# Selective scan and quantized MLP on one core: second-half states added on GpSimd, whole-row peak and square, gating behind the scan, five more products on VectorE

## The chip, the core and the metric

The kernel runs on one core of a Trainium2 chip. A core has five engines that run their own instruction streams and meet only at semaphores: TensorE (PE in the profile), VectorE (DVE), ScalarE (ACT), GpSimd (POOL) and SyncE (SP, which issues the DMAs). The metric is the device time of one execution in microseconds. The lower, the better.

## The reference, cut to what matters

The kernel computes one gated cross-attention-like block. `x` has 4 batches of 512 rows and 512 columns. First a Mamba layer reads a context, then a quantized gated MLP follows:

```python
# Mamba: state [d_inner = 512, 16] for each batch, 512 time steps
def step(state, inp):
    d, b, c, u = inp
    dA = jnp.exp(d[..., None] * A)
    state = state * dA + (d * u)[..., None] * b[:, None, :]
    y = jnp.einsum('bdn,bn->bd', state, c)
    return (state, y)
...
# MLP of 2048 columns; each row is scaled by its RMS and its largest magnitude
xn = rmsnorm(x)
scale = 127.0 / jnp.clip(jnp.max(jnp.abs(x), axis=-1, keepdims=True), EPS, None)
...
h = jax.nn.silu(bitlinear(x, w1)) * bitlinear(x, w2)
return bitlinear(h, w3)
```

`bitlinear` rounds its input rows to integers from -128 to 127 and its weights to -1, 0 and 1. For the third product each row of `h` therefore needs its largest magnitude and its mean square.

## The kernel before, in words

**Steps.** The scan is cut into 128 steps, 32 for each batch, numbered k. A step is a tile `hh[k % 6]` of 128 partitions by 1024 elements. In batches 0 and 1 it holds two states over 512 times. In batches 2 and 3 (`SPLIT`) it holds four states over 256 times: the first 16 steps of such a batch (k = 64 to 79 and 96 to 111) do the first half of the time, the last 16 (k = 80 to 95 and 112 to 127) the second half. Each step passes through these operations:

1. `times_b` on GpSimd (L702, L708): `hh` = (d·u)·B. It waits until TensorE has consumed step k-6 (`s_sum`), since `hh` has six buffers.
2. `exp` on ScalarE (L736, L743): the decay into one of two PSUM tiles `da`, after the scan of step k-2 has freed it.
3. `scan` on VectorE (L763 to L774): the recurrence along the free dimension. In a first half, column 0 of each state's decay is zero, so one instruction of 1024 elements handles four states. In a second half the state at the middle of the time must come in: `keep_state` on ScalarE has copied it into `hl`, and the scan is four instructions of 256 elements, each with its own initial value from `hl` (L770).
4. `times_c` on GpSimd (L813, L818): `hh` = `hh`·C. For the steps in `BY_VECTOR` the scan writes into `da` instead and VectorE multiplies (`times_c_vector`, L796); `exp` of step k+2 then waits for that product.
5. `sums` on TensorE (L851): eight transposes that add into `bank_y`.

**Order.** Every engine's order is written out by hand in slots k. In slot k, GpSimd does `times_c(k)` and `times_b(k+4)`, VectorE does `scan(k+3)`, ScalarE `exp(k+4)`, TensorE `sums(k-1)`.

**MLP tiles.** The 16 row tiles of the MLP start at the slots of `TILE` (38, 44, 50, 56, 70, 76, 82, ..., 118 for the first 13). From slot `tile_slot(i)` on, TensorE makes chunk c (512 of 2048 columns) in slot +c: `a_tensor` (L1020) waits until VectorE has read the chunk before out of `bank_a`, `b_tensor` (L1029) until it has read `bank_b`. In slot +c+1, ScalarE takes a tanh (L1041) and VectorE does two instructions (`gated_vector`, L1048 and L1054), which before stand **ahead of** the slot's scan. ScalarE squares chunks 0 and 1 in slot +2 and chunks 2 and 3 in slot +4 (L1059) and turns each into a part of the mean square `v2` (L1068). VectorE takes the largest magnitudes in the same two halves (L1093). GpSimd raises `v2` to the power -1/2 in slot +7 (`rh_pool`, L1127). VectorE derives the two scales from it (`scales_vector`, L1106 to L1116) and ScalarE rounds `h` (L1123). Tiles 13 to 15 run after the last slot, with code of their own.

Of the kernel before, what the change touches and what calls it, by code (L numbers as in the profile page):

```python
# [13 lines left out]
P = 128  # L14
# [48 lines left out]
BY_VECTOR = (14, 16, 25, 45, 49, 53, 62, 67, 68, 73, 77)  # L63
# [30 lines left out]
def build(nc, book, x, ctx_t, in_w, xp_w, dt_w, weights, consts, out):  # L94
    u_dram = nc.dram_tensor("u_scratch", [NB, P, NE, L], F32).ap()
    xd_dram = nc.dram_tensor("xd_scratch", [NB, ROWS, L], F32).ap()
    with ExitStack() as ctx:
# [23 lines left out]
        sm = sb("sm", [P, 282])  # L121
# [53 lines left out]
        col = iter(range(282))  # L175
# [18 lines left out]
        am1, ram1, rh, rk_most, rk_am, csh = [small() for _ in range(6)]  # L194
# [18 lines left out]
        HA = line("state_scalar")  # L213
# [7 lines left out]
        hl = sb("hl", [P, NE, NS])  # L221

# [466 lines left out]
        def times_b(g_, k):  # L689
# [6 lines left out]
            if split(k):  # L696
                b, h, q, n = where_split(k)
                t = slice(HALF * h, HALF * (h + 1))
                if h == 0 and q == 0:
# [4 lines left out]
                                           [P, 4, HALF]), bb[:, n:n + 4, t], ALU.mult)  # L704
            else:
# [4 lines left out]
            ins.then_inc(s_m1, 1)  # L710

        def exp(act, k, parts=(0, 1)):
# [16 lines left out]
            if split(k):  # L729
                b, h, q, n = where_split(k)  # L730
                da = quarters(flat(dbank[k % 2]))
                if 0 in parts and (k % PER < 2 or h == 0 and c_by_vector(k - 2)):
                    act.activation(da[:, :, 0], zero4[:, :], ACT.Copy)
                first = 1 - h
                for j in [2 * part + i for part in parts for i in range(2)]:
                    ins = act.activation(da[:, j, first:HALF],  # L736
                                         dt2[g % 4][:, HALF * (q % 2) + first:HALF * (q % 2 + 1)], ACT.Exp,
                                         scale=a_neg[:, q, n + j:n + j + 1])
# [6 lines left out]
            if 1 in parts:  # L745
                ins.then_inc(s_exp, 1)

# [10 lines left out]
        def scan(v, k):  # L758
# [297 lines left out]
        def square_scalar(act, i, c):  # L1056

            act.wait_ge(*MV.of(("h", i, c)))
            MA.did(act.activation(view(room, 4096, 1024), h_at(i)[:, c - 1:c + 1, :].rearrange("p a b -> p (a b)"),  # L1059
                                  ACT.Square, accum_out=ssq[:, c // 2:c // 2 + 1]), ("sq", i, c))  # L1060
            act.wait_ge(*MA.now())
            if c == 1:
                act.wait_ge(*MA.of(("k2", rows_by(i))))
            mean_square(act, i, c // 2, c == 3)
# [26 lines left out]
        def peak_vector(v, i, half):  # L1091
            v.wait_ge(*MV.of(("h", i, 2 * half + 1)))
            MV.did(v.tensor_reduce(amh[:, half:half + 1], h_at(i)[:, 2 * half:2 * half + 2, :].rearrange(  # L1093
                "p a b -> p (a b)"), AX.X, ALU.max, apply_absolute_value=True), ("peak", i, half))

        def v2_at(i):
            return ssv[:, 2:3] if at_end(i) else ssv[:, 1:2]

        def scales_vector(v, i, part):
            t = i % NE  # L1100
            if part == 0:
                v.wait_ge(*MV.of(("peak", i, NCH - 1 if at_end(i) else 1)))
                if at_end(i):
                    MV.did(v.tensor_scalar(am1, amh[:, 0:1], amh[:, 1:2], amh[:, 2:3], ALU.max, ALU.max))
                else:
                    MV.did(v.tensor_scalar(am1, amh[:, 0:1], amh[:, 1:2], None, ALU.max))  # L1106
# [108 lines left out]
        def out_vector(v, i):  # L1215
            t = i % NE
            v.wait_ge(*MP.of(("o", i)))
            MV.did(v.scalar_tensor_tensor(out=x2_at(i), in0=bank_g(i)[:, :], scalar=fin[i % 2], in1=x2_at(i),
# [10 lines left out]
        with nc.Block() as block:  # L1229
# [147 lines left out]
            def _(g_):  # L1377
# [37 lines left out]
                for k in range(80, SLOTS):  # L1415
                    for i in range(END):
                        if k == tile_slot(i) + 7:
                            rh_pool(g_, i)
                    if k < ALL and not c_by_vector(k):
                        times_c(g_, k)  # L1420
                    for first, n, done in TURNS:
# [5 lines left out]
                rh_pool(g_, 12)  # L1427
# [16 lines left out]
            def _(act):  # L1444
# [62 lines left out]
                for k in range(38, 80):  # L1507
# [24 lines left out]
                    for i in range(END):  # L1532
                        if k == tile_slot(i) + 7:
                            hq_scalar(act, i, 0)
                            hq_scalar(act, i, 1)
                    for i in range(END):
                        if k == tile_slot(i) + 2 or k == tile_slot(i) + 4:
                            square_scalar(act, i, k - tile_slot(i) - 1)
# [12 lines left out]
                    for first, n, done in TURNS:  # L1551
                        if k == done + 5:
                            rows_scalar(act, first, min(n, END - first))
                            if first + n > END:
                                rows_scalar(act, END, 1)
                for k in range(80, SLOTS):
# [3 lines left out]
                    for i in range(END):  # L1560
                        c = k - tile_slot(i) - 1
                        if 0 <= c < NCH:
                            tanh_scalar(act, i, c)
                    if k + LEAD < ALL:
                        exp(act, k + LEAD)
                    if k + LEAD - 2 < ALL:
# [8 lines left out]
                    for i in range(END):  # L1575
                        if k == tile_slot(i) + 7:
                            hq_scalar(act, i, 0)
                            hq_scalar(act, i, 1)
                    for i in range(END - 1):
# [10 lines left out]
                    for i in range(END):  # L1590
                        if k == tile_slot(i) + 2 or k == tile_slot(i) + 4:
                            square_scalar(act, i, k - tile_slot(i) - 1)
# [9 lines left out]
                    for b in range(NB):  # L1602
                        if k == (13, 34, 66, 94)[b]:
                            z_scales(act, b)
                act.preload_act_table_set("silu_and_others")
# [427 lines left out]
```

## Time and profile before

| | us |
|---|---|
| median of 3 runs | 653.23 (653.22 to 656.8) |
| the profiled execution: its own time | 653.69 |
| its span, first to last instruction | 651.9 |
| DVE busy in the span | 583.0 (89%) |
| ACT busy | 530.7 (81%) |
| POOL busy | 587.9 (90%) |
| PE busy | 488.3 (75%) |

The profile is of one execution. "Busy" is the time in which an engine had an instruction under way. A wait is the idle time just ahead of an instruction, put down to the event that came last. The page also follows the chain of work that ended last; it gives 30% of the span to POOL, 29% to DVE, 14% to ACT and 11% to PE. POOL's record begins its dense part at 26.93 us and ends its last `times_c` at 607.66 us.

### The profile page before, as it was taken

The numbers are of one execution on the slowest core, as the hardware profiler recorded it, in microseconds if no ns is written. First come the engines' busy times: TensorE is split into PE (matmuls) and PEld (weight loads), VectorE is DVE, ScalarE is ACT, GpSimd is POOL, SyncE is SP. The second block draws the span as 40 slices with busy tenths as digits, with TensorE's granted clock in tenths as the row PEclk, the third lists the DMA queues.
The fourth block names the chain that finished last, engine by engine and source line by source line (L and its number), as shares of the span: only waits on it lengthen the run. The fifth ranks groups of instructions, "written<-read, shape, count | busy, mean of one in ns | idle before, by whom it ended". The sixth has DMA issues, their size and how long they took to land.

```text
span 651.9 us, 7928 instructions
## 1 busy us (share of the span) xinstructions
PE 488.3 (75%) x2560; PEld 296.4 (45%) x2560; DVE 583.0 (89%) x772; ACT 530.7 (81%) x969; POOL 587.9 (90%) x289
## 2 busy tenths in 40 slices
PE   8798878994564678777666486778676887668987
PEld 3254434552553445455534354455454554345543
DVE  6779779997998899999999999989997999999765
ACT  5764767788999778987798797899999898897675
POOL 1399999998999999999999999999999999999431
PEclk9988999997555979999786889889989897978999
DMA  5598587579960100147420100037700000000001
GB/s 186 193 407 309 183 329 276 198 270 389 374 262 0 39 1 2 47 153 276 132 78 0 33 2 17 1 127 244 254 37 1 17 1 18 0 16 18 1 17 48
DMA packets 24472, 80.77 MB, mean 124 GB/s; under 512 B 2464, under 2 KB 5152, under 8 KB 21360
## 3 DMA queue, kind: packets, MB, share of 16 engines
q1 hardware_dynamic: 24432, 80.27, 33.9%
q8 instruction: 20, 0.33, 0.2%
q14 instruction: 20, 0.16, 0.1%
HBM read 72.53 MB, written 7.73 MB: 123 GB/s over the span
## 4 chain that ended last, share of the span: by engine, by line
POOL 30%; DVE 29%; ACT 14%; issue 13%; PE 11%; DMA 2%; SPq 0%; DVEq 0%; POOLq 0%; ACTq 0%
POOL hh L708 15%; POOL hh L818 14%; DVE hh L773 9%; DVE hh L770 8%; DVE room L1048 4%; ACT da L736 3%; DVE sm L1093 2%; PE bank_a L1020 2%; PE bank_b L1029 2%; PE bank_y L851 2%; ACT room L1041 1%; PE da L1211 1%; DVE bank_y L576 1%; DVE sm L904 1%; ACT gbuf L922 1%
## 5 line engine op out<-in xcount | busy, mean ns | idle before, releaser
L773 DVE TENSOR_TENSOR_SCAN hh<-da,hh 128x1024 f32<-128x1024 f32 x85 | 193.4, 2280 | 3.1 <-ACT da L743 3.0
L851 PE MATMUL bank_y<-ident,hh 128*128 128x128 f32 x1024 | 145.3, 292 | 10.8 <-POOL hh L818 8.8
L851 PEld LDWEIGHTS bank_y<-ident,hh 128*128 128x128 f32 x1024 | 129.6, 152 | 40.1 <-issue 17.5
L813 POOL TENSOR_TENSOR hh<-hh,cc 128x1024 f32<-128x1024 f32 x60 | 141.0, 2350 | 0.2 <-ACT hl L756 0.2
L818 POOL TENSOR_TENSOR hh<-hh,cc 128x1024 f32<-128x1024 f32 x57 | 134.2, 2355 | 0.0
L708 POOL TENSOR_TENSOR hh<-pair,bb 128x1024 f32<-128x1024 f32 x30 | 70.5, 2352 | 26.4 <-DMA bb<-xd_scratch 24.2
L770 DVE TENSOR_TENSOR_SCAN hh<-da,hl,hh 128x256 f32<-128x256 f32 x128 | 85.4, 729 | 0.0
L708 POOL TENSOR_TENSOR hh<-wq,bb 128x1024 f32<-128x1024 f32 x32 | 75.3, 2357 | 1.8 <-PE bank_y L851 1.8
L702 POOL TENSOR_TENSOR hh<-wq,bb 128x1024 f32<-128x1024 f32 x32 | 75.1, 2346 | 0.3 <-PE bank_y L851 0.3
L702 POOL TENSOR_TENSOR hh<-pair,bb 128x1024 f32<-128x1024 f32 x32 | 75.2, 2355 | 0.0
L736 ACT ACTIVATE da<-wq,cst 128x256 f32<-128x256 f32 x128 | 53.3, 463 | 12.0 <-DVE hh L770 11.6
L743 ACT ACTIVATE da<-pair,cst 128x511 f32<-128x511 f32 x64 | 41.3, 679 | 23.3 <-DVE hh L773 23.3
L1020 PE MATMUL bank_a<-wq,room 128*128 128x512 fp8e4 x120 | 34.2, 412 | 30.2 <-DVE room L1048 27.4
L736 ACT ACTIVATE da<-pair,cst 128x255 f32<-128x255 f32 x128 | 53.0, 459 | 3.5 <-DVE hh L773 3.4
L743 ACT ACTIVATE da<-wq,cst 128x511 f32<-128x511 f32 x64 | 41.4, 682 | 9.4 <-DVE hh L773 9.2
L1020 PE MATMUL bank_a<-wq,xqT 128*128 128x512 fp8e4 x112 | 32.4, 417 | 21.7 <-DVE room L1048 21.7
L1041 ACT ACTIVATE room<-bank_a,sm 128x512 f32<-128x512 f32 x58 | 39.0, 673 | 9.0 <-PE bank_a L1020 8.9
L1211 PE MATMUL bank_t<-wq,room 128*128 128x512 fp8e4 x192 | 45.0, 389 | 0.1
L1048 DVE SCALAR_TENSOR_TENSOR room<-room,bank_a 128x512 f32<-128x512 f32 x52 | 35.2, 677 | 8.0 <-ACT room L1041 7.6
L1029 PE MATMUL bank_b<-wq,room 128*128 128x512 fp8e4 x120 | 34.1, 411 | 0.0
L1190 ACT ACTIVATE room<-bank_t,sm 128x1024 bf16<-128x1024 f16 (+1 forms) x28 | 30.4, 1085 | 4.4 <-PE bank_t L1173 4.4
L987 PE MATMUL bank_t<-ident,room 128*128 128x128 f16 x56 | 6.1, 238 | 34.2 <-ACT room L969 17.4
(271 smaller groups left out, 1051.7 us busy)
## 6 DMA issues: line engine op xcount, KB each, us to landing
bb<-xd_scratch SPq DMA_DIRECT2D x32, 512.0 KB, 5.1
cc<-xd_scratch SPq DMA_DIRECT2D x32, 512.0 KB, 6.9
wq<-weights SPq DMA_DIRECT2D x12, 1024.0 KB, 6.5
stage<-weights SPq DMA_DIRECT2D x8, 1024.0 KB, 6.1
xin<-x SPq DMA_DIRECT2D x4, 1024.0 KB, 5.4
room<-weights SPq DMA_DIRECT2D x4, 1024.0 KB, 8.2
u_scratch<-wq SPq DMA_DIRECT2D x6, 512.0 KB, 3.0
wq<-x SPq DMA_DIRECT2D x2, 1024.0 KB, 18.8
```

The source lines that it names most:

```text
L702: ins = g_.tensor_tensor(quarters(flat(hh[k % NH])), du2[g % 4][:, HALF * (q % 2):HALF * (q % 2 + 1)].unsqueeze(1).to_broadcast([P, 4, HAL ...
L708: ins = g_.tensor_tensor(hh[k % NH][:, :, :], du2[g % 4].unsqueeze(1).to_broadcast([P, GN, L]), bb[:, s * GN:(s + 1) * GN, :], ALU.mult)
L736: ins = act.activation(da[:, j, first:HALF], dt2[g % 4][:, HALF * (q % 2) + first:HALF * (q % 2 + 1)], ACT.Exp, scale=a_neg[:, q, n + j:n ...
L743: ins = act.activation(dbank[k % 2][:, j, 1:L], dt2[g % 4][:, 1:L], ACT.Exp, scale=a_neg[:, q, s * GN + j:s * GN + j + 1])
L770: ins = v.tensor_tensor_scan(to[:, t], da[:, t], h[:, t], hl[:, q, n + j:n + j + 1], ALU.mult, ALU.add)
L773: ins = v.tensor_tensor_scan(to, da, h, 0.0, ALU.mult, ALU.add)
L813: ins = g_.tensor_tensor(quarters(flat(hh[k % NH])), quarters(flat(hh[k % NH])), cc[:, n:n + 4, t], ALU.mult)
L818: ins = g_.tensor_tensor(hh[k % NH][:, :, :], hh[k % NH][:, :, :], cc[:, s * GN:(s + 1) * GN, :], ALU.mult)
L851: mm = pe.matmul(bank_y[:, (first + c) * P:(first + c + 1) * P], flat(hh[k % NH])[:, at:at + P], ident[:, :], start=False, stop=(s == STEP ...
L1020: mm = pe.matmul(a[:, :], xqT[i % 2][:, k, :], w1q[:, k, c * 512:(c + 1) * 512], start=(k == 0), stop=(k == NE - 1))
L1048: MV.did(v.scalar_tensor_tensor(out=th[c % 2], in0=th[c % 2], scalar=1.0, in1=a[:, :], op0=ALU.add, op1=ALU.mult), ("g", i, c))
L1211: mm = pe.matmul(bank_g(i)[:, :], hqT[:, f, :], w3q[:, f, :], start=(f == 0), stop=(f == KF - 1))
```

## The change

In the steps of a second half the scan becomes one instruction of 1024 elements, as in a first half. The state from the middle of the time is brought in ahead of it: ScalarE computes `gain`, the decay of the first column, once for each split batch (`state_gain`, 4 instructions of 128x16, kept in a part of `ones`); GpSimd multiplies `hl` by it once for each group of 128 channels (`carried`, 4 in a batch) and adds the four values of a step to the first column of each state in `hh` (`add_state`, 16 in a batch). It is now `add_state`, and no longer `times_b`, that lets the scan go. Column 0 of the decay is zero throughout, and ScalarE computes 255 columns where it computed 256.

Peak and square of tiles 0 to 12 are one instruction of 2048 elements each, in slot +4. `rh_pool` moves from slot +7 to +6. Two small products move from VectorE to ScalarE (`rk_scalar`, `fin_scalar`), and VectorE makes the scale with three instructions instead of six. `gated_vector` stands behind the scan of its slot. Five steps more (42, 58, 90, 104, 117) have their product by C on VectorE.

```diff
-BY_VECTOR = (14, 16, 25, 45, 49, 53, 62, 67, 68, 73, 77)
+BY_VECTOR = (14, 16, 25, 42, 45, 49, 53, 58, 62, 67, 68, 73, 77, 90, 104, 117)
...
+        gain = ones[:, 0:NE * NS].rearrange("p (e n) -> p e n", e=NE)
...
+                if h:
+                    HG.did(ins, ("product", k))
+                    return
...
+        def carried(g_, k):
+            b, h, q, n = where_split(k)
+            if n == 0:
+                g_.wait_ge(*HA.of(("gain", b)))
+                g_.wait_ge(*HA.of(PER * b + 4 * q + 3))
+                HG.did(g_.tensor_tensor(hl[:, q, :], hl[:, q, :], gain[:, q, :], ALU.mult), ("carried", k))
+
+        def add_state(g_, k):
+            b, h, q, n = where_split(k)
+            g_.wait_ge(*HG.of(("product", k)))
+            first = quarters(flat(hh[k % NH]))[:, :, 0]
+            g_.tensor_tensor(first, first, hl[:, q, n:n + 4], ALU.add).then_inc(s_m1, 1)
...
+        def state_gain(act, b):
+            if b == SPLIT[0]:
+                act.wait_ge(*WP.of("total"))
+            else:
+                act.wait_ge(*HG.of(("carried", PER * (b - 1) + PER - 4)))
+            for q in range(NE):
+                g = NE * b + 2 + q // 2
+                ins = act.activation(gain[:, q, :], a_neg[:, q, :], ACT.Exp,
+                                     scale=dt2[g % 4][:, HALF * (q % 2):HALF * (q % 2) + 1])
+            HA.did(ins, ("gain", b))
...
-            if split(k) and where_split(k)[1]:
-                b, _, q, n = where_split(k)
-                for j in range(4):
-                    t = slice(HALF * j, HALF * (j + 1))
-                    ins = v.tensor_tensor_scan(to[:, t], da[:, t], h[:, t], hl[:, q, n + j:n + j + 1],
-                                               ALU.mult, ALU.add)
-            else:
-                ins = v.tensor_tensor_scan(to, da, h, 0.0, ALU.mult, ALU.add)
-            ins.then_inc(s_scan, 1)
+            v.tensor_tensor_scan(to, da, h, 0.0, ALU.mult, ALU.add).then_inc(s_scan, 1)
...
-        def square_scalar(act, i, c):
+        def square_scalar(act, i):
+            act.wait_ge(*MV.of(("h", i, NCH - 1)))
+            MA.did(act.activation(view(room, 4096, 1024).bitcast(BF16), h_all(i), ACT.Square,
+                                  accum_out=ssq[:, 0:1]), ("sq", i))
...
+        def peak_vector(v, i):
+            v.wait_ge(*MV.of(("h", i, NCH - 1)))
+            MV.did(v.tensor_reduce(am1, h_all(i), AX.X, ALU.max, apply_absolute_value=True), ("peak", i))
...
+        def rk_scalar(act, i):
+            act.wait_ge(*MG.of(("rh", i)))
+            MA.did(act.activation(rk, rh, ACT.Copy, scale=kk[:, i % NE:i % NE + 1]), ("rk", i))
+
+        def scale_vector(v, i):
+            v.wait_ge(*MV.of(("peak", i)))
+            v.wait_ge(*MA.of(("rk", i)))
+            MV.did(v.tensor_scalar(hm, am1, rk, 1e-5, ALU.mult, ALU.max), ("hm", i))
+            v.wait_ge(*MV.now())
+            MV.did(v.reciprocal(hinv, hm))
+            v.wait_ge(*MV.now())
+            MV.did(v.tensor_scalar(csh, hinv, rk, 127.0, ALU.mult, ALU.mult), ("csh", i))
...
@@ GpSimd, slots 80 and on
-                        if k == tile_slot(i) + 7:
+                        if k == tile_slot(i) + 6:
                             rh_pool(g_, i)
                     if k < ALL and not c_by_vector(k):
                         times_c(g_, k)
+                    if second_half(k + LEAD - 1):
+                        add_state(g_, k + LEAD - 1)
+                    if second_half(k + LEAD):
+                        carried(g_, k + LEAD)
...
@@ VectorE, slots 38 and on
+                    if k + LEAD - 1 < ALL:
+                        scan(v, k + LEAD - 1)
                     for i in range(END):
                         c = k - tile_slot(i) - 1
                         if 0 <= c < NCH:
                             gated_vector(v, i, c)
-                    if k + LEAD - 1 < ALL:
-                        scan(v, k + LEAD - 1)
```

In ScalarE's slots from 80 on, a step of `BY_VECTOR` now has its state kept ahead of the `exp` that waits for it, and not behind.

The order of GpSimd in slots 81 to 83, where tile 5 (slot 76) has its `rh_pool`. Before (L702 is `times_b`, L813 `times_c`, L1127 `rh_pool`):

```order
L813 TENSOR_TENSOR hh<-hh,cc 128x1024 [waits s_scan]
L702 TENSOR_TENSOR hh<-wq,bb 128x1024 [waits s_sum]
L813 TENSOR_TENSOR hh<-hh,cc 128x1024 [waits s_scan]
L702 TENSOR_TENSOR hh<-wq,bb 128x1024 [waits s_sum]
L1127 TENSOR_TENSOR sm<-sm 128x1 [waits s_mlp_scalar]
L813 TENSOR_TENSOR hh<-hh,cc 128x1024 [waits s_scan]
```

With the change (L704 `times_b`, L837 `times_c`, L732 `add_state`, L1167 `rh_pool`), slots 81 and 82:

```order
L837 TENSOR_TENSOR hh<-hh,cc 128x1024 [waits s_scan]
L732 TENSOR_TENSOR hh<-hh,hl 128x4 [waits s_state_pool]
L704 TENSOR_TENSOR hh<-wq,bb 128x1024 [waits s_sum]
L1167 TENSOR_TENSOR sm<-sm 128x1 [waits s_mlp_scalar]
L837 TENSOR_TENSOR hh<-hh,cc 128x1024 [waits s_scan]
L732 TENSOR_TENSOR hh<-hh,hl 128x4 [waits s_state_pool]
```

Each slot has a small addition more, behind the product by C, and `rh_pool` stands a whole slot (two large products) earlier.

The order of VectorE in slot 116, the fourth chunk of tile 11. Before (L1048 and L1054 are `gated_vector`, L770 the scan, L1093 the peak, L1218 `out_vector`):

```order
L1048 SCALAR_TENSOR_TENSOR room<-room,bank_a 128x512
L1054 TENSOR_TENSOR wq<-room,bank_b 128x512
L770 SCALAR_TENSOR_TENSOR hh<-da,hl,hh 128x256 x4
L1093 TENSOR_REDUCE sm<-wq 128x1
L1218 SCALAR_TENSOR_TENSOR room<-bank_t,sm,room 128x512
```

With the change:

```order
L798 SCALAR_TENSOR_TENSOR hh<-da,hh 128x1024
L1072 SCALAR_TENSOR_TENSOR room<-room,bank_a 128x512
L1078 TENSOR_TENSOR wq<-room,bank_b 128x512
L1119 TENSOR_REDUCE sm<-wq 128x1
L1260 SCALAR_TENSOR_TENSOR room<-bank_t,sm,room 128x512
```

The scan is one instruction and comes first; the two gating instructions follow it.

## Rows read from the trace of the kernel before

**Rows 1.** The page, parts 1 and 2: whole span, busy tenths of 40 slices.

```profile
PE 488.3 (75%) x2560; PEld 296.4 (45%) x2560; DVE 583.0 (89%) x772; ACT 530.7 (81%) x969; POOL 587.9 (90%) x289
...
POOL 1399999998999999999999999999999999999431
```

**Rows 2.** 20 us each: busy PE, PEld, DVE, ACT, POOL; clock, DMA share, GB/s.

```profile
280.00:300.00 20.00, 16.21 (x106) 10.36 (x106) 19.76 (x23) 15.98 (x25) 20.00 (x10) 1.00 0.54 185
...
560.00:580.00 20.00, 13.27 (x73) 8.03 (x72) 19.19 (x37) 16.53 (x38) 20.00 (x11) 0.83 0.03 13
```

**Rows 3.** Waits of POOL, whole span: us in total, times, longest.

```profile
POOL hh L708 <- DMA bb<-xd_scratch: 24.2, 1, 24.2
POOL sm L1127 <- ACT sm L1068: 20.5, 3, 8.3
POOL hh L708 <- PE bank_y L851: 4.0, 3, 1.8
```

**Rows 4.** Timeline of POOL: start, us, instruction, idle before it in brackets.

```profile
574.24 0.53 POOL L1127 TENSOR_TENSOR sm<-sm 128x1 f32<-128x1 f32 x1
574.74 2.34 POOL L813 TENSOR_TENSOR hh<-hh,cc 128x1024 f32<-128x1024 f32 x1
```

**Rows 5.** POOL by line and form: busy us, mean ns of one, idle before.

```profile
L1127 POOL TENSOR_TENSOR sm<-sm 128x1 f32<-128x1 f32 x16 | 8.6, 540 | 20.5 <-ACT sm L1068 20.5
L1133 POOL TENSOR_SCALAR room<-room,sm 128x1024 f16<-128x1024 f32 x3 | 3.4, 1119 | 1.0 <-DVE sm L1115 0.8
...
L928 POOL TENSOR_TENSOR sm<-sm 128x4 f32<-128x4 f32 x2 | 2.0, 1008 | 0.0
L1141 POOL TENSOR_SCALAR wq<-wq,sm 128x512 f16<-128x512 f32 x2 | 1.4, 692 | 0.9 <-DVE sm L1115 0.8
...
L1379 POOL MEMSET wq<- 128x3 f32 x4 | 0.2, 100 | 0.3 <-POOLq L2027 0.3
```

**Rows 6.** DVE by line and form.

```profile
L773 DVE TENSOR_TENSOR_SCAN hh<-da,hh 128x1024 f32<-128x1024 f32 x85 | 193.4, 2280 | 3.1 <-ACT da L743 3.0
L770 DVE TENSOR_TENSOR_SCAN hh<-da,hl,hh 128x256 f32<-128x256 f32 x128 | 85.4, 729 | 0.0
L1048 DVE SCALAR_TENSOR_TENSOR room<-room,bank_a 128x512 f32<-128x512 f32 x52 | 35.2, 677 | 8.0 <-ACT room L1041 7.6
...
L796 DVE TENSOR_TENSOR hh<-da,cc 128x1024 f32<-128x1024 f32 x11 | 13.5, 1225 | 0.4
...
L1115 DVE TENSOR_SCALAR sm<-sm 128x1 f32<-128x1 f32 x16 | 3.4, 214 | 0.6
```

**Rows 7.** ACT by line and form.

```profile
L1068 ACT ACTIVATE sm<-sm 128x1 f32<-128x1 f32 x35 | 13.5, 387 | 1.2
...
L623 ACT ACTIVATE wq<-wq 128x2048 f32<-128x2048 f32 x4 | 7.6, 1904 | 0.0
```

**Rows 8.** Timeline of DVE, end of tile 9's last chunk.

```profile
511.31 2.28 DVE L773 TENSOR_TENSOR_SCAN hh<-da,hh 128x1024 f32<-128x1024 f32 x1
```

**Rows 9.** Timeline of ACT, tile 9's second square.

```profile
511.42 1.06 ACT L1059 ACTIVATE room<-wq 128x1024 f32<-128x1024 f32 x1 [0.28 <-DVE wq L1054]
...
512.61 0.39 ACT L1068 ACTIVATE sm<-sm 128x1 f32<-128x1 f32 x1
```

**Rows 10.** Timeline of POOL beside it.

```profile
512.38 2.35 POOL L813 TENSOR_TENSOR hh<-hh,cc 128x1024 f32<-128x1024 f32 x1
...
517.03 0.53 POOL L1127 TENSOR_TENSOR sm<-sm 128x1 f32<-128x1 f32 x1
```

**Rows 11.** Timeline of PE, chunk 1 of tile 7.

```profile
439.86 1.04 PE L1020 MATMUL bank_a<-wq,xqT 128*128 128x512 fp8e4 x4 [1.31 <-DVE room L1048]
...
441.60 1.04 PE L851 MATMUL bank_y<-ident,hh 128*128 128x128 f32 x8
```

**Rows 12.** Timeline of POOL beside it.

```profile
440.95 2.36 POOL L813 TENSOR_TENSOR hh<-hh,cc 128x1024 f32<-128x1024 f32 x1
443.27 2.35 POOL L702 TENSOR_TENSOR hh<-wq,bb 128x1024 f32<-128x1024 f32 x1
```

More of the change, by code:

```diff
@@ L174, in build @@
         gates = cst[:, 92:94]
-        col = iter(range(282))
+        col = iter(range(285))
         def small(n=1):
@@ L193, in build @@
         ssq, ssv, amh = [small(3) for _ in range(3)]
-        am1, ram1, rh, rk_most, rk_am, csh = [small() for _ in range(6)]
+        am1, ram1, rh, rk, rk_most, rk_am, hm, hinv, csh = [small() for _ in range(9)]
         fin = [small() for _ in range(2)]
@@ L1089, in peak_end, with fin_scalar @@
                    ("peak", i, c))
[L1091 to L1094, printed above, removed]
+        def peak_vector(v, i):
+            v.wait_ge(*MV.of(("h", i, NCH - 1)))
+            MV.did(v.tensor_reduce(am1, h_all(i), AX.X, ALU.max, apply_absolute_value=True), ("peak", i))
         def v2_at(i):
-            return ssv[:, 2:3] if at_end(i) else ssv[:, 1:2]
+            return ssv[:, 2:3] if at_end(i) else ssv[:, 0:1]
+        def rk_scalar(act, i):
[9 more added lines that the diff above has]
+            MV.did(v.tensor_scalar(csh, hinv, rk, 127.0, ALU.mult, ALU.mult), ("csh", i))
+        def fin_scalar(act, i):
+            act.wait_ge(*MV.of(("hm", i)))
+            MA.did(act.activation(fin[i % 2], hm, ACT.Copy, scale=g3d), ("fin", i))
         def scales_vector(v, i, part):
@@ L1101, in scales_vector @@
             if part == 0:
[L1102 to L1106, printed above, removed]
+                v.wait_ge(*MV.of(("peak", i, NCH - 1)))
+                MV.did(v.tensor_scalar(am1, amh[:, 0:1], amh[:, 1:2], amh[:, 2:3], ALU.max, ALU.max))
                 v.wait_ge(*MV.now())
@@ L1217, in out_vector @@
             v.wait_ge(*MP.of(("o", i)))
+            if not at_end(i):
+                v.wait_ge(*MA.of(("fin", i)))
             MV.did(v.scalar_tensor_tensor(out=x2_at(i), in0=bank_g(i)[:, :], scalar=fin[i % 2], in1=x2_at(i),
@@ L1590, in _ @@
                     for i in range(END):
-                        if k == tile_slot(i) + 2 or k == tile_slot(i) + 4:
-                            square_scalar(act, i, k - tile_slot(i) - 1)
+                        if k == tile_slot(i) + 4:
+                            square_scalar(act, i)
+                    for i in range(END):
+                        if k == tile_slot(i) + 6:
+                            rk_scalar(act, i)
                     for i in TILES:
@@ L1884, in _ @@
                             rows_vector(v, first, n)
-                    for i in range(END):
-                        if k == tile_slot(i) + 5:
-                            scales_vector(v, i, 0)
                     for first, n, done in TURNS:
@@ L1906, in _ @@
                             du_vector(v, 2 * n + 1)
-                    for i in range(END):
-                        if k == tile_slot(i) + 2:
-                            peak_vector(v, i, 0)
                 for k in range(80, SLOTS):
@@ L1921, in _ @@
                                 aggr_vector(v, i)
+                    if k + LEAD - 1 < ALL:
+                        scan(v, k + LEAD - 1)
                     for i in range(END):
@@ L1925, in _ @@
                             gated_vector(v, i, c)
-                    if k + LEAD - 1 < ALL:
-                        scan(v, k + LEAD - 1)
-                    for i in range(END):
-                        if k == tile_slot(i) + 5:
-                            scales_vector(v, i, 0)
                     for first, n, done in TURNS:
```

67 lines of the change are left out of this document (40 added, 27 removed).

## Prediction

> **What bounds the kernel now.** Read the page's busy line and its slices first. POOL is busy 90% of the span, but that is no average of a half idle engine: after the start its slices stand at 9 until the last three [rows 1]. The table by stretch shows 20.00 us of 20 for POOL, with DVE at 19.2 to 19.8 and ACT at 16.0 to 16.5 [rows 2]. Then read POOL's waits: 24.2 us once, at the start, for the first rows of B; 20.5 us in three waits for ScalarE's mean squares, which are those of the last three tiles, after the scan; and 4.0 us for TensorE [rows 3]. So from 27 us to 608 us GpSimd issues one large product after another, every 2.32 us (from 440.95 to 443.27) [rows 12], and the end of that stream releases the last sums, from which the tail of some 44 us is counted. The time is the sum of GpSimd's instructions in the dense part, plus its waits. VectorE is nearly as full, though. The chain that ended last passes through it, and it leads GpSimd by a few us only. Less work on DVE alone therefore buys nothing, and less on POOL buys something only as long as DVE keeps its lead.
>
> **The change, on GpSimd.** Removed: five products by C, 5 x 2.32 = 11.6 us. Added: 32 additions of 128x4 and 8 products of 128x16. The trace has no small addition, so it is bounded. From below, by the memset of 128x3, 0.10 us [rows 5]. From above, by the power of 128x1, which takes 0.50 us from start to start (574.24 to 574.74) [rows 4]; that one is mostly the power itself, since four elements take 1008 ns against 540 for one, 0.16 us an element, which leaves 0.38 us fixed [rows 5]. The one-input operation with a pointer scalar takes 1119 ns for 1024 elements and 692 for 512: 0.27 us fixed [rows 5]. An addition needs no pointer scalar and no power routine, but reads two operands; I take 0.20 us, between the memset and that 0.27, nearer to the latter. Then 32 x 0.20 = 6.4 us, and 8 x 0.22 = 1.8 us. Net on POOL: -11.6 + 8.2 = **-3.4 us**. With 0.10 us it is -7.6, with 0.50 it is +8.4.
>
> The Trainium skill (GPSIMD Engine Reference, Elementwise — side-by-side cycle accounting) gives 4497 ns for a two-input addition of 2048 elements. Against the 2.32 us that 1024 elements take here, this leaves an estimated 0.14 us fixed; the additions would come to 5.6 us and the net to -6.0.
>
> **On VectorE.** A second-half scan takes 85.4/32 = 2.67 us in four pieces and 2.28 in one [rows 6]: 32 x 0.39 = -12.5. The scales shrink from six tiny operations to three, at about 0.2 us each (214 ns) [rows 6]: 13 x 0.6 = -7.8. One peak of 2048 for two of 1024 I count as nothing. Five products at 1.225 us [rows 6] add 6.1. Sum -14 us. None of it shows in the time by itself; it enlarges VectorE's lead. It is unevenly spread: up to slot 80 there is no second half, and DVE gets two products (+2.5) against six tiles' scales (-3.6), while GpSimd is relieved of 4.6.
>
> **On ScalarE.** Two squares of 1.06 us with their reading and scaling (0.39 each) become one of 1.90 us (the 2048-wide one) [rows 7, 9]; `rk`, `fin` and eight small exponentials take about that much again. ACT has 3.5 us of 20 idle [rows 2], so zero, apart from the moment at which things are ready.
>
> **The moved steps and what they wait for.** Two moves work against the gain.
>
> First, `gated_vector` behind the scan frees `bank_a` one scan, 2.3 us, later. TensorE is already waiting there (1.31 us before 439.86), and what is queued behind is the sums that free `hh`: in tile 7 they run from 441.60 to 442.64, and GpSimd takes the buffer at 443.27 [rows 11, 12]. Only 0.6 us is left, and 2.3 us more would stall POOL by 1.7, unless DVE's lead has grown by as much. Against this, VectorE no longer stands idle for ScalarE's tanh (7.6 us in all) [rows 6].
>
> Second, `rh_pool` comes a slot earlier while its mean square comes later. Take tile 9: its last chunk will be complete where the scan ends now, at 513.6 [rows 8]; then a square of 1.90, its accumulator read and the scaling of 0.39, some 2.6 us in all, gives 516.2 [rows 7, 9]. GpSimd is at the place where `rh_pool` will stand at 512.38, whereas today it comes to it at 517.03 [rows 10]. At today's relative position it would wait 3.8 us. But such a wait shifts GpSimd once: afterwards it runs that much later behind VectorE, and the next tile finds its value ready, as long as VectorE keeps the lead. VectorE's 12.5 us in second halves supply it, and POOL's additions do too. In slots 38 to 80 there is no such supply; I price the loss there at 2 us, about one shift of the lead, less what the vanished waits for tanh return.
>
> Sum: -3.4 + 2 = -1.4 us. The profiled execution took 653.69, its span 651.9 and 1.8 around it; it stands 0.5 above the median. Against the median of 653.2 the forecast is **651.8 us**.
>
> **The rivals.**
>
> 1. *Cheap additions, and the waits swallowed.* With 0.10 us each and no new wait the sum is -7.6: 645.6. For it: the memset's row, and the idle places of DVE that vanish. Against it: only 0.6 us of slack on the sums. A cost between, near -6, gives 647. Chance 0.25.
>
> 2. *The early `rh_pool` and late square bind in tile after tile.* GpSimd waits in front of `rh_pool` for ScalarE, with `times_c`, `add_state` and so the scan of three steps later behind it. It decides where VectorE's lead can't reach the 3.8 us that tile 9 asks for, because the scan now waits for `add_state`, which comes a product (2.3 us) later than `times_b` did; GpSimd and VectorE then hold each other. Half of that deficit, 1.9 us, on six of the eight tiles from slot 76 on is +11: 653.2 - 3.4 + 11 = 661. For it: the rows of tile 9. Against it: the lead is lost only by product moves, three in that part. Chance 0.12.
>
> 3. *Dear additions.* At 0.40 us the added work is 32 x 0.40 + 8 x 0.42 = 16.2 us, the net +4.6, with the 2 us of waits 659.8. For it: the fixed 0.38 of the power. Chance 0.10.
>
> 4. *The relief cancels.* Moving a product changes the lead by 2.3 + 1.2 = 3.5 us each time, and VectorE becomes the bound up to slot 80, so the first two products give nothing: -3.4 + 4.6 = +1.2, or 654.4. Chance 0.15.
>
> **How the numbers follow.** The forecast has 0.38 of the chance. A measurement here tells about 1% (6.5 us) from no change. Faster by more than that, below 646.7, takes most of rival 1 and a little of the forecast's price range: 0.22. Slower, above 659.8, takes rival 2 and half of rival 3: 0.17. Within: 0.61. The range reaches from rival 1 (645.5) to dear additions with some waits, 659.5.
>
> **What would show it.** Each step in the profile of the changed kernel: POOL's rows for the 128x4 additions (0.20 us apart from start to start); POOL still at 20 of 20 us in stretches from 30 to 600, while DVE falls to about 18 in the second halves; waits of POOL on `bank_y` (sums) and on ScalarE's mean square of a few us before 600, not more than 4 in all; VectorE's waits for the tanh gone; the last `times_c` at about 606 in place of 607.7. The prediction is wrong if the additions take under 0.1 or over 0.4 us, or if POOL shows more than 6 us of new waits ahead of `rh_pool` or `times_b`.

## The result

The changed kernel takes 689.9 us (median of 4 runs, 688.2 to 693.5) against 653.2 before: the ratio is 1.053, with a 95% interval of 1.050 to 1.057. By the ratio it is slower by 35 us, and it lies far above the range that was given. One of the four executions of rh_late, a run told below, took 724.8 us at a granted TensorE clock of 0.71, where its others had 0.87; it is left out.

**The profile after.** The page's busy line and POOL's slices, which answer to [rows 1]:

```profile
PE 502.5 (73%) x2560; PEld 304.3 (44%) x2560; DVE 572.0 (83%) x629; ACT 530.3 (77%) x969; POOL 583.3 (85%) x324
...
POOL 1499999998999698798998799998997799999521
```

VectorE is busy 11.0 us less than before, where 14 was summed, and GpSimd 4.6 us less, where 3.4 was; the span is 34.5 us longer. The three stretches that show it, two of them those of [rows 2] (busy us of PE, PEld, DVE, ACT, POOL; clock; DMA):

```profile
core 0: us, PE busy (x) PEld busy (x) DVE busy (x) ACT busy (x) POOL busy (x), PEclk, DMA share, GB/s
220.00:240.00 20.00, 13.66 (x76) 9.05 (x74) 16.81 (x15) 9.98 (x16) 14.14 (x7) 0.83 0.08 26
280.00:300.00 20.00, 14.80 (x100) 9.43 (x100) 17.43 (x16) 16.44 (x23) 16.51 (x9) 1.00 0.31 106
560.00:580.00 20.00, 14.16 (x80) 8.85 (x80) 17.20 (x17) 14.90 (x31) 20.00 (x15) 0.91 0.03 13
```

In two of the three GpSimd is no longer full: 14.1 and 16.5 us of 20. Where it went is in the waits of POOL, over the whole span, against [rows 3]:

```profile
POOL sm L1167 <- ACT sm L1094: 29.9, 8, 8.3
POOL hh L713 <- DMA bb<-xd_scratch: 23.8, 1, 23.8
POOL hh L713 <- PE bank_y L875: 18.2, 8, 5.9
POOL hh L704 <- PE bank_y L875: 14.1, 8, 4.9
```

The waits for `bank_y` (TensorE's sums) have gone from 4.3 to 32.3 us, those for the mean square from 20.5 to 29.9. VectorE has new waits too:

```profile
DVE bank_y L578 <- PE bank_y L875: 17.7, 8, 4.7
DVE gbuf L532 <- ACT bank_a L526: 14.2, 10, 2.3
DVE hh L798 <- POOL hh L732: 8.3, 7, 2.6
```

`L578` is the y gate, the product of the finished sums with the gated z, which comes every eight slots. It waits 17.7 us for the sums. Before, from 200 to 600 us, it waited 0.7 there. GpSimd's account closes: 28.0 (sums) + 9.4 (mean square) + 1.8 (other) of new waits, less 4.6 of work, is 34.6 us, and the last `times_c` ends at 642.3 in place of 607.7.

**What was right.** The prices of the added work, which the trace before did not have:

```profile
L732 POOL TENSOR_TENSOR hh<-hh,hl 128x4 f32<-128x4 f32 x32 | 6.5, 203 | 0.2
...
L726 POOL TENSOR_TENSOR hl<-hl,ones 128x16 f32<-128x16 f32 x8 | 1.8, 224 | 0.0
```

0.203 us for an addition, where 0.20 was taken, and 0.224 for a product of 128x16, where 0.22 was. The scan and the peak:

```profile
L798 DVE TENSOR_TENSOR_SCAN hh<-da,hh 128x1024 f32<-128x1024 f32 x112 | 254.6, 2280 | 14.8 <-POOL hh L732 8.3 <-ACT da L764 5.1 <-ACT da L757 0.6
...
L1072 DVE SCALAR_TENSOR_TENSOR room<-room,bank_a 128x512 f32<-128x512 f32 x52 | 34.6, 665 | 2.7 <-ACT room L1065 2.6
...
L1119 DVE TENSOR_REDUCE sm<-room 128x1 f32<-128x2048 f32 x7 | 16.0, 2283 | 0.2
```

The second-half scan takes 2.28 us in one piece, and the wait for the tanh at the gating (L1072) has fallen from 7.6 to 2.6 us. Both were forecast. None of it shows in the time, because the engines now wait for each other.

**The loop.** This is the chain of waits in the slots 39 and 40 (start, duration, engine and line), as the chain that ended last has it:

```profile
216.84 1.18 DVE da L798
...
219.05 0.69 DVE room L1072
...
219.78 1.04 PE bank_a L1044 x4
220.82 0.86 PE bank_b L1053 x4
221.68 0.89 PE bank_y L875 x8
...
222.59 0.71 DVE bank_y L578
...
224.00 2.28 DVE hh L798
226.28 0.59 DVE room L1072
...
226.92 1.89 PE bank_a L1044 x4
228.81 1.71 PE bank_b L1053 x4
230.52 1.67 PE bank_y L863 x8
232.18 0.87 PE bank_y L875 x8
```

Read it downwards. The chain gives an instruction only the part that counts in it: the first scan lasts 2.30 us on VectorE. When it ends, the gating (L1072) starts at 219.05, and only that frees `bank_a`. TensorE makes the two MLP products (L1044, L1053), and behind them, in its queue, the sums of slot 39 (L875). The y gate (L578) needs those sums, and scan and gating of slot 40 stand behind the y gate. So the next `bank_a` is free only at 226.87. TensorE, which waited 4.4 us for it, makes two products, the products that start the next group's `bank_y` (L863) and the sums of slot 40, until 233.1. GpSimd wants the buffer of those sums for `times_b`:

```profile
224.92 2.36 POOL L713 TENSOR_TENSOR hh<-pair,bb 128x1024 f32<-128x1024 f32 x1
233.14 2.36 POOL L713 TENSOR_TENSOR hh<-pair,bb 128x1024 f32<-128x1024 f32 x1 [5.86 <-PE bank_y L875]
```

It idles 5.86 us. The same happens in slot 72, where the y gate again meets a tile's second chunk (4.87 us at 381.01).

One link more lies in these rows. The four products for `bank_a` take 1.04 us at 219.78 and 1.89 us at 226.92, after TensorE has idled 4.37 us. The granted clock (third figure from the end) was 1.00 from 216 to 222 us and has fallen to 0.50, the lower of its two levels, during that idle time:

```profile
226.90:229.00 2.10, 2.08 (x5) 0.74 (x6) 2.10 (x2) 0.15 (x1) 0.38 (x1) 0.50 0.00 0
229.00:232.00 3.00, 3.00 (x12) 2.33 (x11) 2.74 (x4) 1.73 (x3) 0.00 (x0) 0.50 0.00 0
```

So the sums come later still. In the kernel before, the products of the same slot, at 221.55, took 1.04 us after 0.73 us of idling. Of the five longest waits of GpSimd for the sums from 200 to 600 us, four (at 233.14, 313.39, 381.01 and 465.59, 16.2 us in all) have such a stretch at 0.50 just ahead of them, and one (3.49 us at 284.39) has none, though TensorE had idled 3.62 us there. At 1.00 the two MLP products and the sums take 2.61 us from the start of the first to the start of what follows (at 281.53). At 226.92 the two MLP products and those of L863 take 5.10 us in its place; at 309.23 and 461.42 the first three groups take 3.87 and 3.92, and at 375.82 all four take 4.95 in place of some 3.48. So I estimate that the lower clock makes 6.5 of those 16.2 us. The mean granted clock from 200 to 600 us is 0.90 before and 0.86 with the change. No run holds the clock fixed, so its part in the 35 us is not shown.

### The profile page after: what moved, and what is told of

Its sections match the earlier page's. It is cut to its first block, busy times and chain, and to the rows that moved or that the text cites. A ratio compares the mean times of both kernels' runs of the same rounds, so it can differ in the third digit from the quotient of the medians.

```text
span 686.4 us, 7829 instructions
## 1 busy us (share of the span) xinstructions
PE 502.5 (73%) x2560; PEld 304.3 (44%) x2560; DVE 572.0 (83%) x629; ACT 530.3 (77%) x969; POOL 583.3 (85%) x324
## 4 chain that ended last, share of the span: by engine, by line
DVE 22%; PE 21%; POOL 18%; issue 17%; ACT 16%; DMA 4%; SPq 1%; DVEq 0%; POOLq 0%; ACTq 0%
POOL hh L704 9%; DVE hh L798 9%; POOL hh L837 7%; PE bank_y L875 3%; PE bank_a L1044 3%; PE bank_b L1053 3%; DMA wq<-x 3%; DVE room L1072 2%; ACT da L764 2%; ACT da L757 2%; PE bank_b L258 2%; DVE da L798 2%; PE bank_t L270 1%; ACT wq L681 1%; PE bank_a L258 1%
## 5 line engine op out<-in xcount | busy, mean ns | idle before, releaser
L798 DVE TENSOR_TENSOR_SCAN hh<-da,hh 128x1024 f32<-128x1024 f32 x112 | 254.6, 2280 | 14.8 <-POOL hh L732 8.3
L875 PE MATMUL bank_y<-ident,hh 128*128 128x128 f32 x1024 | 148.8, 296 | 11.1 <-POOL hh L842 9.0
L875 PEld LDWEIGHTS bank_y<-ident,hh 128*128 128x128 f32 x1024 | 133.3, 155 | 43.4 <-issue 21.0
L837 POOL TENSOR_TENSOR hh<-hh,cc 128x1024 f32<-128x1024 f32 x57 | 134.4, 2359 | 2.0 <-ACT hl L788 2.0
L842 POOL TENSOR_TENSOR hh<-hh,cc 128x1024 f32<-128x1024 f32 x55 | 129.8, 2361 | 0.0
L704 POOL TENSOR_TENSOR hh<-pair,bb 128x1024 f32<-128x1024 f32 x32 | 75.5, 2362 | 8.8 <-PE bank_y L875 8.8
L704 POOL TENSOR_TENSOR hh<-wq,bb 128x1024 f32<-128x1024 f32 x32 | 75.4, 2356 | 5.3 <-PE bank_y L875 5.3
L1044 PE MATMUL bank_a<-wq,room 128*128 128x512 fp8e4 x120 | 39.3, 460 | 40.8 <-DVE room L1072 36.5
L764 ACT ACTIVATE da<-pair,cst 128x511 f32<-128x511 f32 x64 | 41.3, 680 | 20.5 <-DVE hh L798 20.5
L757 ACT ACTIVATE da<-wq,cst 128x255 f32<-128x255 f32 x128 | 53.3, 467 | 2.0 <-DVE hh L798 2.0
L1044 PE MATMUL bank_a<-wq,xqT 128*128 128x512 fp8e4 x112 | 33.3, 425 | 21.3 <-DVE room L1072 20.9
L1251 PE MATMUL bank_t<-wq,room 128*128 128x512 fp8e4 x192 | 43.4, 379 | 0.8 <-ACT room L1230 0.8
L1053 PE MATMUL bank_b<-wq,room 128*128 128x512 fp8e4 x120 | 38.9, 457 | 0.0
L798 DVE TENSOR_TENSOR_SCAN da<-da,hh 128x1024 f32<-128x1024 f32 x16 | 36.6, 2288 | 1.5 <-ACT da L764 1.2
L1072 DVE SCALAR_TENSOR_TENSOR room<-room,bank_a 128x512 f32<-128x512 f32 x52 | 34.6, 665 | 2.7 <-ACT room L1065 2.6
L1044 PEld LDWEIGHTS bank_a<-wq,room 128*128 128x128 bf16 x120 | 11.5, 110 | 55.3 <-DVE room L1072 40.1
```

What stands on the lines that cost most here:

```text
L704: ins = g_.tensor_tensor(quarters(flat(hh[k % NH])), du2[g % 4][:, HALF * (q % 2):HALF * (q % 2 + 1)].unsqueeze(1).to_broadcast([P, 4, HAL ...
L757: ins = act.activation(da[:, j, 1:HALF], dt2[g % 4][:, HALF * (q % 2) + 1:HALF * (q % 2 + 1)], ACT.Exp, scale=a_neg[:, q, n + j:n + j + 1])
L764: ins = act.activation(dbank[k % 2][:, j, 1:L], dt2[g % 4][:, 1:L], ACT.Exp, scale=a_neg[:, q, s * GN + j:s * GN + j + 1])
L798: v.tensor_tensor_scan(to, da, h, 0.0, ALU.mult, ALU.add).then_inc(s_scan, 1)
L837: ins = g_.tensor_tensor(quarters(flat(hh[k % NH])), quarters(flat(hh[k % NH])), cc[:, n:n + 4, t], ALU.mult)
L842: ins = g_.tensor_tensor(hh[k % NH][:, :, :], hh[k % NH][:, :, :], cc[:, s * GN:(s + 1) * GN, :], ALU.mult)
```

## The experiments

All times are medians, beside runs of the kernel before on the same chip, whose median was 655.3 to 655.8 there. Ratios are to those, with 95% intervals.

| kernel | us | ratio |
|---|---|---|
| gate_ahead | 659.4 | 1.007 (1.004 to 1.010) |
| rh_late | 692.1 | 1.055 (1.052 to 1.058) |
| both_undone | 658.9 | 1.005 (1.003 to 1.007) |
| before_gate_behind | 691.3 | 1.053 (1.051 to 1.056) |
| behind_sums_first | 667.1 | 1.017 (1.013 to 1.022) |
| before_sums_first | 667.9 | 1.021 (1.016 to 1.025) |
| after_sums_first | 670.9 | 1.025 (1.022 to 1.027) |
| state_only | 663.3 | 1.012 (1.009 to 1.016) |
| undone_old_products | 662.6 | 1.011 (1.008 to 1.015) |
| before_early_two | 656.6 | 1.003 (1.001 to 1.005) |
| undone_late_three | 657.4 | 1.003 (1.001 to 1.006) |
| undone_late_six | 654.7 | 1.000 (0.998 to 1.001) |
| behind_to_80 | 672.6 | 1.027 (1.024 to 1.030) |
| behind_from_80 | 672.9 | 1.027 (1.023 to 1.030) |
| state_late_six | 653.7 | 0.997 (0.995 to 0.999) |
| behind_gate_last | 664.0 | 1.013 (1.010 to 1.017) |
| before_gate_last | 657.3 | 1.003 (1.001 to 1.005) |
| state_six_gate_last | 656.8 | 1.001 (0.999 to 1.003) |

### Which of the moves

gate_ahead: the changed kernel with

```diff
+                    for i in range(END):
+                        c = k - tile_slot(i) - 1
+                        if 0 <= c < NCH:
+                            gated_vector(v, i, c)
                     ...
                     if k + LEAD - 1 < ALL:
                         scan(v, k + LEAD - 1)
-                    for i in range(END):
-                        c = k - tile_slot(i) - 1
-                        if 0 <= c < NCH:
-                            gated_vector(v, i, c)
```

> The changed kernel with the two gating instructions ahead of the slot's scan again; all else as changed. Theory 1 (the gating behind the scan frees bank_a one scan late, TensorE's sums queue behind that wait, and GpSimd's times_b waits for the sums, 32 us in all in the changed profile against 4 before): most of it returns, 660 to 665 us, and GpSimd's waits for bank_y fall under 8 us. Theory 2 (the early power of the late mean square holds GpSimd and the rest follows): stays at 685 or more. Theory 3 (the five products on VectorE make it the bound): stays within 5 us of 690.

rh_late: the changed kernel with

```diff
-                        if k == tile_slot(i) + 6:
+                        if k == tile_slot(i) + 7:
                             rh_pool(g_, i)
```

and `rk_scalar` at the head of ScalarE's slot +7.

> The changed kernel with GpSimd's power of the mean square in slot +7 again, and ScalarE's small product of it at the head of slot +7; gating stays behind the scan. Theory 1: 9 us of waits ahead of the power go, but they are partly taken over by waits for the sums, 680 to 687 us. Theory 2: falls to 665 or below.

both_undone has both edits.

> The changed kernel with both moves undone: gating ahead of the scan and the power in slot +7. The state on GpSimd, the one-piece peak and square and the five products stay. Theory 1 with 2: no new waits on GpSimd, its sum of -3.4 us shows, 649 to 655 us. If it stays above 660, the one-piece square or the products carry a cost of their own (theory 3).

before_gate_behind: the kernel before with the gating behind the scan, and nothing else.

```diff
-                    for i in range(END):
-                        c = k - tile_slot(i) - 1
-                        if 0 <= c < NCH:
-                            gated_vector(v, i, c)
                     ...
                     if k + LEAD - 1 < ALL:
                         scan(v, k + LEAD - 1)
+                    for i in range(END):
+                        c = k - tile_slot(i) - 1
+                        if 0 <= c < NCH:
+                            gated_vector(v, i, c)
```

> The kernel before with nothing changed but the gating behind the scan. Theory 1: this edit alone costs 20 us or more, 673 to 682 us, with GpSimd waiting 20 us or more for bank_y. If the gating only hurts together with the later release of the scan by add_state (theory 2's lock of GpSimd and VectorE), it stays under 660 us.

Theory 1 held, and its size was underrated: before_gate_behind was expected at 673 to 682 us and took 691.3. The gating alone costs 5.3% on the kernel before, as much as the whole change, and putting it back takes 30 of 35 us away. The early power is no loss to speak of: putting it back gives nothing while the gating stays behind (1.055 against 1.053, where 680 to 687 us was expected), and 0.5 us once it is ahead. So its waits of 9.4 us in the changed kernel did not add to the time; most likely GpSimd would otherwise have waited for the sums there. The square stays late in both runs; it is taken up with undone_old_products. In before_gate_behind the waits of POOL, and that of the y gate on DVE, from 200 to 640 us are:

```profile
POOL hh L702 <- PE bank_y L851: 20.1, 8, 5.1
POOL hh L708 <- PE bank_y L851: 13.1, 4, 5.6
```

```profile
DVE bank_y L576 <- PE bank_y L851: 18.4, 7, 3.8
```

That is 33.2 us of GpSimd for the sums and 18.4 us of VectorE for them. both_undone missed its expectation of 649 to 655 by 4 us; that remainder is taken up below.

### By way of TensorE's queue

behind_sums_first: before_gate_behind, with TensorE's order changed as follows (the head of the slot loses its sums, but for step 37 in slot 38).

```diff
-                    if 0 <= k - 1 < ALL:
-                        sums(pe, k - 1)
...
+                    if k < ALL - LEAD:
+                        sums(pe, k)
                     for i in range(END + 1):
                         c = k - tile_slot(i)
                         if 0 <= c < NCH:
                             a_tensor(pe, i, c)
```

> The kernel before with the gating behind the scan, and with TensorE's sums of step k in slot k ahead of the slot's first MLP product, instead of at the head of slot k+1 behind both. Theory 1a (the loss is that the sums queue on TensorE behind a product that waits for the gating): GpSimd's waits for bank_y vanish and most of the 35 us come back, 655 to 662 us. Theory 1b (the later bank_a delays ScalarE's tanh, and with it the exponentials behind it, whatever the sums do): stays above 675 us.

before_sums_first: the same on the kernel before, with gating ahead.

> The kernel before with that move of the sums alone. GpSimd waited only 4 us for the sums, so both theories expect no change, within 3 us of 655; a rise above 660 would mean that the MLP products need their place ahead of the sums.

after_sums_first: the same on the changed kernel.

> The changed kernel with the sums of step k ahead of the slot's first MLP product on TensorE; gating stays behind the scan. On the kernel before, this took the gating's 35 us down to nothing beside the move's own 12. If the loss of the changed kernel is the same one (theory 1a), it falls from 690 to 665 to 670 us. If the changed kernel has a lock of its own (the scan let go by add_state, the early power), it stays above 675.

These close a square. With the sums behind the MLP products, the gating's place makes 655 or 691; with the sums ahead of them, 668 or 667. So at least 24 of the 36 us that the gating's place costs come through the sums that queue behind the product which waits for it (theory 1a). That it costs nothing at all with the sums ahead is not shown: a smaller loss by another way could hide behind the 12 us that the next paragraph tells of. The changed kernel likewise falls from 690 to 671.

behind_sums_first ended above its expected 655 to 662, for a reason that its control shows: moving the sums costs 12 us on its own, where before_sums_first was expected within 3 us of 655. Now the MLP products stand behind sums that wait for GpSimd, and the chain tanh, gating gets late. In before_sums_first, from 200 to 615 us:

```profile
DVE room L1048 <- ACT room L1041: 20.8, 17, 3.1
```

```profile
ACT room L1041 <- PE bank_a L1020: 24.1, 13, 4.9
```

VectorE waits 20.8 us for the tanh, where the kernel before, over its whole span, waited 7.6 [rows 6], and ScalarE 24.1 us for the MLP product, where it waited 6.5 from 200 to 615 us.

### Why it comes back

behind_to_80 and behind_from_80: the edit of before_gate_behind in one of VectorE's two loops over slots only.

> The kernel before with the gating behind the scan in slots 38 to 79 only, where six tiles run. If each tile pays anew (the loss recurs), about 6/13 of the 35 us, 667 to 674 us. If the wait is a single shift, as the prediction had it, at most 659.

> The same in slots from 80 on only, where seven tiles run. If each tile pays anew, 671 to 678 us, and the two halves' losses add up to some 35 us. If the loss needs the long run of tiles, the two add up to much less.

The halves cost 16.9 and 17.1 us by the medians, and add up to 34 of the 36 us of before_gate_behind. The loss recurs; it is not a shift paid once.

behind_gate_last: before_gate_behind with the y gate behind the gating.

```diff
-                    if k % STEPS == 0 and PER < k <= ALL:
-                        gate(v, k // STEPS - 1)
                     if k + LEAD - 1 < ALL:
                         scan(v, k + LEAD - 1)
                     ...
                             gated_vector(v, i, c)
+                    if k % STEPS == 0 and PER < k <= ALL:
+                        gate(v, k // STEPS - 1)
```

> The kernel before with the gating behind the scan, and with the y gate (which comes every 8 slots and waits for the sums of the slot before) moved from the slot's head to behind the gating. Theory G (the wait recurs because the y gate hands TensorE's lateness back to VectorE: sums wait for the gating, the y gate for the sums, and scan and next gating stand behind it): more than half of the 35 us returns, 672 us or less, and VectorE's 16 us of waits for bank_y shrink. Theory S (each chunk pays for the scan's length by itself): at most 5 us return, 685 us or more.

before_gate_last: the kernel before, with the y gate just behind the scan.

> The control: the kernel before with the y gate behind the scan, gating ahead of both as before. VectorE waited 0.7 us there, so neither theory expects more than 2 us either way: 653 to 658 us.

Theory G held. 27 of the 36 us come back, with the gating still behind the scan. The control stays within 2 us of the kernel before. GpSimd's waits for the sums from 200 to 640 us have fallen from 33.2 to 9.1:

```profile
POOL hh L702 <- PE bank_y L851: 4.6, 4, 2.7
POOL hh L708 <- PE bank_y L851: 4.5, 2, 3.9
```

VectorE's waits for the sums at the y gate have fallen from 18.4 to 0.8 us. So the y gate, ahead of scan and gating, is the link that hands TensorE's lateness back to VectorE. The edit also takes its two instructions (L578 and L593 in the changed kernel, 0.70 and 0.69 us) out from ahead of the gating, once in eight slots; no run tells this from the wait. Some 8 us stay with the gating behind the scan even so (664.0 against 655.5), and the 9.1 us of waits above, where the kernel before had 0.3, are of that size. The longest, 3.93 us at 279.18, stands behind a product for `bank_a` that waited 3.85 us for the gating, 18 us after the last y gate began.

### The added work and the products

state_only: the kernel before with `state_gain`, `carried`, `add_state` and the scan in one piece; no product is moved.

> The kernel before with only the state brought in by GpSimd: 32 additions at 0.20 us and 8 products at 0.22 more on GpSimd, which is full, and 12.5 us less on VectorE. If GpSimd's sum sets the time, it costs 8 us: 660 to 665 us. If VectorE's lead matters as much, under 656.

663.3 is 8 us above the kernel before (1.012, or 6 to 10 us by the interval), for 32 x 0.20 + 8 x 0.22 = 8.2 us of work summed; in its trace the additions take 0.216 us and the products 0.234, 8.8 us. From 200 to 615 us this kernel has no wait of GpSimd at all, and VectorE is busy 571.6 us in place of 583.0, less in the second halves (stretches as above):

```profile
280.00:300.00 20.00, 15.13 (x96) 9.51 (x95) 19.76 (x23) 16.11 (x25) 20.00 (x11) 1.00 0.54 181
400.00:420.00 20.00, 12.89 (x73) 8.29 (x74) 18.43 (x28) 17.01 (x34) 20.00 (x16) 0.84 0.04 14
560.00:580.00 20.00, 12.40 (x70) 7.29 (x69) 17.06 (x21) 16.65 (x40) 20.00 (x15) 0.85 0.04 14
```

The rule on which the prediction was built fits it: while GpSimd does not wait, the time follows its sum, and 11.4 us taken off VectorE buy nothing.

undone_old_products: both_undone with the old `BY_VECTOR`.

> The changed kernel with gating ahead, the power in slot +7 and the five products back on GpSimd: what is left is the state on GpSimd and the one-piece peak and square. GpSimd has 11.6 us more than with the five products on VectorE. If its sum sets the time, 658.9 becomes 668 to 671; if the five products were what VectorE could not carry, it stays at 655 to 660.

662.6 against 663.3 for state_only: the one-piece peak and square and the moved small products are worth nothing measurable, as predicted, and the late square costs nothing either. VectorE is busy 565.1 us, 6.5 less than in state_only, and has a new wait. From 200 to 615 us:

```profile
DVE sm L1132 <- ACT sm L1127: 11.3, 9, 3.0
DVE room L1072 <- ACT room L1065: 11.0, 11, 2.4
DVE hh L798 <- POOL hh L732: 6.2, 7, 2.2
```

`L1132` waits 11.3 us for `rk` from ScalarE, which the kernel before did not have. Against both_undone, it also shows what the five products bring: 3.7 us, not 11.6. The expectation by GpSimd's sum (668 to 671) was made from both_undone with its waits: 8.0 us from 200 to 605 us, of which 2.2 are left when GpSimd has its load back.

before_early_two: the kernel before with 42 and 58 added to `BY_VECTOR`. undone_late_three: both_undone without 42 and 58. undone_late_six: both_undone with 84, 90, 104, 109, 115 and 121 as the late ones.

> The kernel before with steps 42 and 58 moved to VectorE, nothing else. GpSimd has 4.6 us less to do, VectorE 2.5 more with 97% of its time taken. If GpSimd's sum decides, 649 to 652 us. If VectorE's lead is used up there (the cancelled relief), 653 us or more, with new waits of GpSimd for bank_y or for the scan before 400 us.

> Both moves undone and of the five products only 90, 104 and 117 on VectorE. If the two early products gave nothing, as their cancelled relief says, this is as fast as with all five, 656 to 659 us, or faster; if they gave their 4.6 us, it is at 662 to 664.

> As the last, with 84, 90, 104, 109, 115 and 121: products from the part in which VectorE has won 12.5 us. GpSimd's sum falls by 6.9 us more. If VectorE's lead carries them, 649 to 653 us, a version faster than both; if each late product brings waits of its own (the exponentials of step k+2 come after the product), 656 us or more.

The two early products bring nothing: 656.6 on the kernel before, and taking them out of both_undone changes 658.9 to 657.4. In before_early_two, GpSimd's 4.6 us of relief come back as waits: 6.7 us between 200 and 605 us, where the kernel before had 0.5.

```profile
POOL hh L708 <- PE bank_y L851: 3.4, 4, 1.8
POOL hh L702 <- PE bank_y L851: 2.6, 2, 2.0
POOL sm L928 <- ACT sm L916: 0.7, 1, 0.7
```

Late products do pay, in part: the six bring undone_old_products from 662.6 to 654.7, 7.9 of their 13.9 us. This version is as fast as the kernel before, and misses its hoped-for 649 to 653.

state_late_six: state_only with the same six late products.

> The kernel before with the state on GpSimd and products 84, 90, 104, 109, 115 and 121 on VectorE; peak, square, scales, gating and the power as before. State alone had 663.3 us and not one wait of GpSimd between 200 and 600 us. GpSimd's sum falls by 6 x 2.32 = 13.9 us: 649 to 652 us if VectorE's lead carries them, faster than both kernels. If the late products bring waits by themselves, 655 us or more; the one-piece square and the small products moved to ScalarE are not in it, so it tells their waits apart from these.

state_six_gate_last: the same with the y gate behind the scan.

> The state on GpSimd with six late products (653.7 us), with the y gate behind the scan. Its GpSimd waits 10 us between 200 and 615 us, 4.5 of it for the sums, its VectorE 3 us for bank_y. If these come through the y gate, 649 to 652 us; if not, 653 to 655.

state_late_six is the fastest kernel of the study, at 0.997 (0.995 to 0.999) of the kernel before: some 2 us of 655.7, clear of noise and small. It leaves out everything that the change did to the MLP tiles. 9.7 of the six products' 13.9 us arrive, which is short of its expectation of 649 to 652; against the rest stand waits that GpSimd did not have in state_only, 6.5 us from 200 to 605 us. Whether another choice of products would bring the rest was not tried. Moving the y gate on it gained nothing: it costs 3 us (656.8 against 653.7), where 649 to 655 was expected. Why is open.

## Why the prediction was wrong

- **What bounds the kernel: right.** GpSimd's sum decides as long as it does not wait, as state_only shows within its interval (6 to 10 us for 8.2 summed), and work off VectorE alone buys nothing.
- **The cost of each piece: right.** 0.203 and 0.224 us; the net of work on GpSimd was -4.6 where -3.4 was summed, that on VectorE -11.0 where -14 was.
- **"But such a wait shifts GpSimd once": this step failed.** The prediction saw both waits, put 1.7 us on the sums in one place of tile 7 and 3.8 on the mean square in tile 9, and then charged 2 us in all, because a late GpSimd would find the next value ready. The term of 2 us measured 39 us of new waits on GpSimd. The argument treats VectorE as free to keep its lead. It is not: the y gate makes VectorE wait for the sums, the sums wait behind products that wait for VectorE's gating, and with the gating behind the scan this loop holds a scan and two products more. The prediction names the y gate nowhere. The shift is paid anew, 17 us in each half of the MLP's slots. Moving the y gate behind the gating returned 27 of 36 us, which shows the link. The prediction also let TensorE's work behind the wait take its usual time; part of it ran at the lower clock (1.89 us in place of 1.04).
- **Which of the two waits: wrong.** Rival 2 forecast the loss on the early power, at 661, with a chance of 0.12. The loss was on the sums: rh_late puts the power back and gains nothing. The rival's form, engines that hold each other, was right; its place was not.
- **The waits for the tanh: right, and beside the point.** They fell by 5 us on VectorE.
- **The five products: half wrong.** Rival 4 (the two early ones cancel) is what before_early_two shows. The late three were taken at their full 7.0 us; undone_late_three against undone_old_products gives 5.2.
- **The range.** It was made from prices of work (8 us either way) and one wait. The price of a reordered queue had no upper end in it.

Open: why the waits for the sums that make the remaining 8 us come where they do, with the y gate out of the loop; what part of the loss is the lower clock; and why moving the sums ahead costs just 12 us.

## What to carry to other kernels

When an instruction is moved behind another on one engine, follow what it frees all the way round: through each queue in which something else stands behind the waiter, until a path returns to the same engine. If it returns, the delay is paid in every turn, and a slack read off in one place says nothing of the total. If the engine that bounds the kernel does not wait, count its instructions, and no other engine's. A cheap experiment is to make a reordering alone on the old kernel.

## What was not expected of the hardware

Beside the granted clock, which fell while TensorE stood idle in one wait of the loop and not in another (4.37 us before 226.92, 3.62 before 281.53), nothing of a size that matters. A GpSimd addition of 128x4, with a step of 256 elements between its columns, took 0.203 us, and a product of 128x16 took 0.224, so that these two small two-input instructions both cost about 0.2 us, beside 2.36 us for 1024 elements. Neither changed GpSimd's large products (2350 ns before, 2359 after), though VectorE's scans beside them went from four pieces to one.
